# The roots of the token blocks by a power on GpSimd, and their decay matmul over split exponents

## The chip, the cores and the metric

The kernel runs on one core of a Trainium2 chip. The metric is the device time of one launch in microseconds (us). The engines are TensorE (PE, with its weight loads as PEld), VectorE (DVE), ScalarE (ACT), GpSimd (POOL) and SyncE (SP). Each follows its own program; they meet only through semaphores.

## The reference, cut to what matters

16 sequences of 256 tokens with 128 features go through four layers. Each layer's output is added to its input and normalized:

```
x = layernorm(x + mamba(x))                # state-space layer, 4 heads of 64, 128 states
x = layernorm(x + gated_expert_attention(x))   # 8 heads of 64, 8 experts, causal
x = layernorm(x + linear_attention(x))     # 16 heads of 8, rotary, gelu
x = layernorm(x + soft_experts(x))         # 64 experts x 32 slots
```

Two pieces of the state-space layer matter here. Its decay is exp of sums of dt * A over the steps between two tokens, and its output is normalized by a root, as are the layer norms:

```
dA = exp(dt * A)
h  = h * dA_t + dt_t * x_t B_t
y  = y * rsqrt(mean(y * y) + 1e-5) * norm_w
layernorm(y) = (y - mean) * rsqrt(var + eps) * w + b
```

## The kernel before, in words

`token_blocks` computes the first three layers; `soft_experts` computes the fourth. Within `token_blocks` a sequence has two chunks of 128 tokens (C = 2). The layers run as a pipeline over the sequences, one "slot" per sequence: slot t works on the state-space layer of sequence t (names with a_), on the attention of t-1 (b_), on its output turn of t-2 and on the linear attention of t-3 (c_). The slots up to 2 are written out by hand as a start, with the constants' loads and the step sizes of all sequences (`dt_steps`) between them. Then come slots 3 to 16. The order of the work on each of the five engines is written out by hand, the same in each slot (from slot 15 on pieces of the next sequence, such as its convolution, are left out, since there is none). Nothing reorders it: an instruction whose semaphores are not there holds all that is behind it on its engine.

The names that the change and the steps of the prediction touch:

- `newton` (L60) computes 1/sqrt of a 128x2 tile, on GpSimd: v = var * scale + eps (L64), an integer seed (L66), then three steps of four instructions (L80, L82, L84, L86). That is 14 instructions, each with a wait for the one before. It is called for `rms` (the state-space norm, from `ssq`), `ln` (twice a slot: ln1 and ln2), `lnB`, `lnC`, `lnD`, six times a slot.
- The decay: `a_all` holds the step exponents (-dt*A) of all sequences. `a_am` on GpSimd (L2208) spreads one chunk's four columns to a masked 128x512 tile `am` in the arena, one affine_select for each chunk. `a_seg` on TensorE (L529) multiplies it with the lower triangle `low_s` in f32, a single 128x512 matmul per chunk, which gives the sums of the exponents; the trace shows it as two records. ScalarE then takes the exponential (L1226).
- `b_vg` on GpSimd (L2225) multiplies the values of the attention by their gates, two passes of 128x512 (`vals`).
- `a_mx` (L2218), `a_xb` (L2235), `c_km` (L2248, L2250) and `c_turn` (L2242) are GpSimd's other work in a slot.
- On VectorE: the convolution taps (L1581, six pairs a slot), the rotary products `c_qr` (L1771, L1776: its output `qr` goes to the transposes L785 on TensorE), the gated output `mo` (L1741), `kv` (L1781, needed by TensorE's L799), the residual `ra` (L1644, which reads the `rms` root), `na` (L389) and `x` (L1664), which read the ln roots.
- `arena` is one SBUF tile in which the a_ work has its areas.

Of the kernel before, what the change touches and what calls it, by code (L numbers as in the profile page):

```python
# [15 lines left out]
P = 128  # L16
# [43 lines left out]
def newton(pool, wait_apart, done, k, source, var, scale, eps, v, y, t, fused=False):  # L60


    wait_apart(pool, source)
    pool.tensor_scalar(v[:], var, scale, eps, ALU.mult, ALU.add).then_inc(done, 1)  # L64
    wait_apart(pool, (done, k + 1))
    pool.tensor_scalar(y[:].bitcast(I32), v[:].bitcast(I32), -0.5, RSQRT_SEED,  # L66
                       ALU.mult, ALU.add).then_inc(done, 1)
    if fused:
        for s in range(RSQRT_STEPS):
            wait(pool, done, k + 2 + 3 * s)  # L70
            pool.scalar_tensor_tensor(t[:], y[:], -0.5, y[:], ALU.mult, ALU.mult).then_inc(done, 1)
            wait(pool, done, k + 3 + 3 * s)
            pool.tensor_tensor(t[:], t[:], v[:], ALU.mult).then_inc(done, 1)
            wait(pool, done, k + 4 + 3 * s)
            pool.scalar_tensor_tensor(y[:], t[:], 1.5, y[:], ALU.add, ALU.mult
                                      ).then_inc(done, 1 if s < RSQRT_STEPS - 1 else 1 + RSQRT_STEPS)
        return
    for s in range(RSQRT_STEPS):
        wait(pool, done, k + 2 + 4 * s)
        pool.tensor_tensor(t[:], y[:], y[:], ALU.mult).then_inc(done, 1)  # L80
        wait(pool, done, k + 3 + 4 * s)
        pool.tensor_tensor(t[:], t[:], v[:], ALU.mult).then_inc(done, 1)  # L82
        wait_apart(pool, (done, k + 4 + 4 * s))
        pool.tensor_scalar(t[:], t[:], -0.5, 1.5, ALU.mult, ALU.add).then_inc(done, 1)  # L84
        wait(pool, done, k + 5 + 4 * s)
        pool.tensor_tensor(y[:], y[:], t[:], ALU.mult).then_inc(done, 1)  # L86


def build(nc, x, xT, in_wT, conv_w, conv_b, dt_bias, A_log, Dh, norm_w, out_wT, ln_w, ln_b,
          w_q, w_k, w_gate, v_exp, o_exp, WqkvT, bq, bk, bv, gamma, beta, phi, W, b_exp,  # L90
          ident, causal, neg_blocks, strict_low, upper, head_of, rot, cosT, sinT, w8,
          out):
    x3_dram = nc.dram_tensor("x3_tok", (NB * L, D), F32, kind="Internal").ap()
    x3T_dram = nc.dram_tensor("x3_T", (D, NB * L), F32, kind="Internal").ap()
    ctx = ExitStack()
# [14 lines left out]
def token_blocks(nc, kept, x, xT, in_wT, conv_w, conv_b, dt_bias, A_log, Dh, norm_w, out_wT, ln_w, ln_b,  # L110
# [3 lines left out]

    HELD = NB - 3

    AREAS = dict(cin=(NCH, L + TAPS - 1), cacc=(NCH, L), xbc=(NCH, L), am=(C, NH, P), lx=(C, NH, P), mx=(C, NH, P),
                 xd=(C, NH, HD), xD=(C, NH, HD), tz=(C, DI), sz=(C, DI), ya=(C, DI), yg=(C, DI), yT=(2, L),
                 xt_in=(2, L), x_in=(2, C, D))
    arena = kept.enter_context(nc.sbuf_tensor("arena", [P, sum(math.prod(shape) for shape in AREAS.values())], F32))  # L120
    area, at = {}, 0
    for name, shape in AREAS.items():
# [13 lines left out]
    with ExitStack() as ctx:  # L136
        def sb(name, shape, dt=F32):
            return ctx.enter_context(nc.sbuf_tensor(name, [P] + shape, dt))
# [2 lines left out]
            return kept.enter_context(nc.semaphore(name))  # L141


        id_f = sb("id_f", [P])
        id_b = sb("id_b", [P], BF16)
        fill = sb("fill", [L], BF16)
        id_r = sb("id_r", [P], F32R)
        causal_s = sb("causal_s", [P])
        negb_f = sb("negb_f", [3, P])
        negb = sb("negb", [3, P], BF16)  # L150
        low_s = sb("low_s", [P])
        upp_s = sb("upp_s", [P])
        hof = sb("hof", [P])
        hof_n = sb("hof_n", [P])
# [3 lines left out]
        sin_s = sb("sin_s", [L])  # L158
        w8_s = sb("w8_s", [NE])
        in_w = sb("in_w", [2 * DI + 2 * D + NH])  # L160
        out_w0 = sb("out_w0", [2, D])
        out_w = sb("out_w", [2, D])
        cw0 = sb("cw0", [NCH, TAPS])
        cb0 = sb("cb0", [NCH])
# [31 lines left out]
        bet = sb("bet", [D])  # L196


        sv = sb("sv", [TT, NH])
        sa = sb("sa", [TT, NH])  # L200
        su = sb("su", [TT, NH])
        sd = sb("sd", [TT, NH])
        s2 = sb("s2", [TT, NH])
        sp = sb("sp", [TT, NH])
        ea = sb("ea", [NH])
        dt_all = sb("dt_all", [TT, NH])
        a_all = sb("a_all", [TT, NH])


        xt_in = area["xt_in"]  # L210
# [4 lines left out]
        xd = area["xd"]  # L215
        xD = area["xD"]
        btok = sb("btok", [P])
        gm = sb("gm", [C, P])
        am = area["am"]
        lx = area["lx"]  # L220
        mx = area["mx"]
        ep = sb("ep", [NH])
# [7 lines left out]
        sq = sb("sq", [DI])  # L230
        ssq = sb("ssq", [C])
        yT = area["yT"]
        ra = sb("ra", [C, D])
        na = sb("na", [C, D])
        xb = sb("xb", [C, D])
        x1 = sb("x1", [C, D])
# [17 lines left out]
        rg = sb("rg", [C, HB])  # L254
        rgS = sb("rgS", [C, 2, DH])
        rgb = sb("rgb", [C, P])
        oT = sb("oT", [2, C, HP, P])

        mo = ve_f[:, 0:MO * HP * P].rearrange("p (s a n) -> p s a n", s=MO, a=HP)
        oa = sb("oa", [L])  # L260
# [91 lines left out]
        CONV_PREP = 4  # L352
        PREP = CONV_PREP + 10
        DT_PARTS = [slice(0, C), slice(C, TT)]
        DT_OPS = LOG1P_TERMS + 10
        DT_TILES = [range(C), range(C, C + 8), range(C + 8, C + 16), range(C + 16, C + 23), range(C + 23, TT)]
        VE_PARTS = 4

# [20 lines left out]

        def rsqrt(pool, n, b, scale, eps, source, per, fused=False):  # L380
            _, _, v, y, t = nbuf[n]
            newton(pool, wait_both, norms[n]["rstd"], RSQRT_OPS * b, (source, per * b + per), var_of(n), scale, eps,
                   v, y, t, fused)

        def scale_rows(dve, n, src, dst, b):

# [85 lines left out]
        def _(pe):  # L472
# [43 lines left out]
            def a_seg(b, c):  # L516

                if c == 0:
                    if b == 1:
                        pe.wait_ge(q["a_r"], C * b)  # L520
                    if b not in (1, 2):
                        pe.wait_ge(q["a_sz"], b + 1)
                    if b > 1:
                        pe.wait_ge(q["a_x1h"], b)
                        pe.wait_ge(q["a_x1l"], b)
                else:
                    pe.wait_ge(q["a_lx"], C * b + 1)
                pe.wait_ge(q["a_am"], C * b + c + 1)
                pe.matmul(ps_a[:, :], low_s[:], am[:, c, :, :].rearrange("p h t -> p (h t)"),  # L529
                          start=True, stop=True, skip_group_check=True).then_inc(q["a_seg_ps"], 1)  # L530

            def a_xt(b):
                pe.wait_ge(q["a_xbc"], b + 1)
# [458 lines left out]
            a_z(0, 0)  # L992
            a_xbc(1, 1, 0, 0)
            pe.wait_ge(ready, READY)
            a_seg(0, 0)
            dt_rows(1)
            a_seg(0, 1)
# [192 lines left out]
        def _(act):  # L1190
# [50 lines left out]
            def a_sq(b):  # L1241

                act.wait_ge(q["a_yg"], b + 1)
                for c in range(C):
                    if c == 1:
                        act.wait_ge(q["a_sq"], C * b + 1)
                    nc.scalar.activation(sq[:], yg[:, c, :], ACT.Square, scale=0.5, accum_out=ssq[:, c:c + 1]
                                         ).then_inc(q["a_sq"], 1)

            def a_yt(b):  # L1250
# [104 lines left out]
            def dt_exps(n):  # L1355
                act.wait_ge(dts, DT_OPS * n + 2)
                nc.scalar.activation(su[:, DT_PARTS[n], :], sa[:, DT_PARTS[n], :], ACT.Exp, scale=-1.0
                                     ).then_inc(dt_exp, 1)

            def slot(r, u, a, b, o, c, more):  # L1360
                t = 2 * r + u
                if a:
# [204 lines left out]
        def _(dve):  # L1567
# [303 lines left out]

            def dt_steps(n):
                rows = DT_PARTS[n]
                dve.wait_ge(dt_exp, n + 2)
                V.tensor_scalar(sd[:, rows, :], su[:, rows, :], 2.0, None, ALU.add).then_inc(dts, 1)
                dve.wait_ge(dts, DT_OPS * n + 3)
                V.reciprocal(sd[:, rows, :], sd[:, rows, :]).then_inc(dts, 1)
# [7 lines left out]
                for k in range(LOG1P_TERMS - 1, 0, -1):  # L1885
# [12 lines left out]
                V.scalar_tensor_tensor(a_all[:, rows, :], dt_all[:, rows, :], -1.0,  # L1898
                                       ea[:].unsqueeze(1).to_broadcast([P, rows.stop - rows.start, NH]), ALU.mult, ALU.mult
                                       ).then_inc(dts, 1)  # L1900
                dve.wait_ge(dts, DT_OPS * n + DT_OPS)

            def slot(r, u, a, b, o, c, more):
                t = 2 * r + u
# [122 lines left out]
            dt_steps(0)  # L2027
            a_conv(0, 0, (2,))
            a_sz(0)
            a_conv(0, 0, (3,))  # L2030
            a_conv(0, 1, (1,))
            a_conv(0, 1, (2,))
# [165 lines left out]
        @block.gpsimd  # L2198
        def _(pool):
            G = nc.gpsimd  # L2200

            def a_am(b):

                if b < 2:
                    pool.wait_ge(dts, DT_OPS * (b + 1))
                for c in range(C):
                    wait(pool, q["a_seg_ps"], C * b)
                    G.affine_select(out=am[:, c, :, :], in_=a_all[:, b * C + c, :].unsqueeze(2).to_broadcast([P, NH, P]),  # L2208
                                    compare_op=ALU.is_ge, fill=0.0, base=0, pattern=[[0, NH], [1, P]],
                                    channel_multiplier=-1).then_inc(q["a_am"], 1)  # L2210

            def a_mx(b):

# [844 lines left out]
```

## Time and profile before

| | before |
|---|---|
| times of three runs | 1496.85, 1499.70, 1500.32 us |
| median | 1499.7 us |
| span of the profiled execution | 1497.5 us |
| PE busy | 1440.1 us (96%) |
| DVE busy | 1218.1 us (81%) |
| ACT busy | 821.0 us (55%) |
| POOL busy | 751.1 us (50%) |
| `token_blocks` / `soft_experts` | up to about 1004 us / the rest |

For the profiled execution only its span is given; no time of its own stands beside it. The span runs from the first to the last instruction. "Busy" counts the time in which an engine computes. PEclk is the TensorE clock that was granted as a share of full speed. A row "idle before <-ENGINE name" says how long an engine sat and what let it go on. In the three runs the time varies by 3.5 us.

### The profile page before, as it was taken

The page shows a single profiled execution, that of the slowest core. Times are in us where ns is not written, and L with a number is a line of the kernel's source. Part 1 is how long each engine was busy: PE and PEld are TensorE (multiplying, and loading weights), DVE is VectorE, ACT ScalarE, POOL GpSimd, SP SyncE. Part 2 cuts the span into 40 slices and gives each one's busy share as a digit, 9 for nine tenths or more (in the row PEclk, how much of TensorE's full clock was granted, in tenths as well). Part 3 has the DMA queues.
Part 4 walks back from the last instruction along what each step waited for, and adds up shares of the span by engine and source line. Part 5 has one row for each costly group of instructions (what it writes and reads, how often), then busy time and mean ns, then how long its engine had stood idle before and what let it go on. Part 6 is the DMA issues. An engine that isn't in the chain of part 4 may idle for free. (4 is left out here: it accounts for less than half of the span.)

```text
span 1497.5 us, 32591 instructions
## 1 busy us (share of the span) xinstructions
PE 1440.1 (96%) x10940; PEld 1269.0 (85%) x10940; DVE 1218.1 (81%) x2359; ACT 821.0 (55%) x1850; POOL 751.1 (50%) x1833
## 2 busy tenths in 40 slices
PE   8889999999999999999999999987999999998998
PEld 6658888888888888888888887867999999998997
DVE  5778889889898898898898887768888888857664
ACT  4354454555454455455554544315777767677775
POOL 1433346355354454453463452226777777457772
PEclk8789999999999999999999999998999999999999
DMA  5100000000000000000000003006777777887872
GB/s 193 60 8 8 1 15 2 15 16 1 15 5 12 15 5 12 15 1 15 16 1 15 9 1 127 1 1 166 188 187 192 196 192 192 263 335 296 310 304 75
DMA packets 135426, 130.43 MB, mean 87 GB/s; under 512 B 7232, under 2 KB 125248, under 8 KB 128768
## 3 DMA queue, kind: packets, MB, share of 16 engines
q1 hardware_dynamic: 135296, 128.79, 27.8%
q8 instruction: 70, 1.15, 0.3%
q14 instruction: 60, 0.49, 0.1%
HBM read 72.93 MB, written 55.84 MB: 86 GB/s over the span
## 5 line engine op out<-in xcount | busy, mean ns | idle before, releaser
L737 PE MATMUL ps_l<-ve_f,oe 128*128 128x128 f32 x2048 | 275.7, 279 | 0.8 <-DVE ve_f L1741 0.8
L737 PEld LDWEIGHTS ps_l<-ve_f,oe 128*128 128x128 f32 x2048 | 248.8, 192 | 23.1 <-issue 20.5
L1741 DVE SCALAR_TENSOR_TENSOR ve_f<-ps_s,oT 128x512 f32<-128x512 f32 x248 | 166.4, 679 | 4.1 <-PE ps_l L737 2.3
L2935 POOL TENSOR_TENSOR d_s<-d_ex 128x1024 f32<-128x1024 f32 x31 | 125.3, 4041 | 83.2 <-ACT d_ex L2685 83.2
L1702 DVE COPY_PREDICATED vals<-oh,ps_l 128x1024 f32<-128x1024 int32 x112 | 146.8, 1311 | 17.2 <-PE ps_l L477 15.1
L2560 PE MATMUL ps_s<-d_ex,arena 128*128 128x128 f32 x1024 | 121.5, 278 | 7.0 <-DVE d_ex L2828 7.0
L2560 PEld LDWEIGHTS ps_s<-d_ex,arena 128*128 128x128 f32 x1024 | 118.7, 194 | 7.4 <-DVE d_ex L2828 7.4
L475 PE MATMUL ps_l<-veH,x1H 128*128 128x512 f32 x256 | 115.4, 451 | 0.8 <-DVE vals L1702 0.7
L1293 ACT ACTIVATE ve_f<-ps_l,r 128x128 f32<-128x128 f32 x128 | 47.3, 369 | 125.7 <-DVE r L1714 125.4
L2548 PE MATMUL ps_l<-arena 128*128 (+1 forms) x960 | 112.2, 275 | 2.3 <-ACT d_raw L2680 2.3
L2548 PEld LDWEIGHTS ps_l<-arena 128*128 128x128 f32 x960 | 109.6, 192 | 2.5 <-ACT d_raw L2680 2.5
L64 POOL TENSOR_SCALAR lnB_v<-lnB_mv 128x2 f32<-128x2 f32 x15 | 2.9, 193 | 213.5 <-DVE lnB_mv L378 213.5
L477 PE MATMUL ps_l<-veH,x1L 128*128 128x512 f32 x256 | 101.0, 395 | 0.0
L476 PE MATMUL ps_l<-veL,x1H 128*128 128x512 f32 x256 | 100.5, 393 | 0.0
L2810 DVE TENSOR_REDUCE d_nm<-ps_l 128x128 f32<-128x2048 f32 x31 | 71.0, 2291 | 32.7 <-PE ps_l L2548 28.5
L1192 ACT ACTIVATE pt<-ps_l 128x384 f32<-128x384 f32 x128 | 62.7, 494 | 62.4 <-PE ps_l L675 61.1
L2737 ACT ACTIVATE e_prT<-ps_l 128x512 f32<-128x512 f32 x128 | 72.5, 595 | 38.8 <-PE ps_l L2603 38.8
L2856 DVE TENSOR_REDUCE e_nmx<-e_lt 128x1 f32<-128x2048 f32 x32 | 73.0, 2282 | 19.1 <-DMA e_lt<-logits 18.1
L1581 DVE SCALAR_TENSOR_TENSOR arena<-arena,cw 128x256 f32<-128x256 f32 x192 | 85.7, 489 | 1.2 <-ACT arena L1192 1.1
L2603 PE MATMUL ps_l<-d_id,e_lt 128*128 128x128 f32 x512 | 77.9, 276 | 6.4 <-ACT e_lt L2729 6.4
L2676 ACT ACTIVATE d_raw<-ps_l 128x512 f32<-128x512 f32 x120 | 67.1, 603 | 20.9 <-DVE d_nm L2810 9.3
L2828 DVE TENSOR_TENSOR d_ex<-d_ex,d_sr 128x2048 f32<-128x2048 f32 x32 | 74.7, 2335 | 1.1
(332 smaller groups left out, 3865.8 us busy)
## 6 DMA issues: line engine op xcount, KB each, us to landing
logits<-d_raw SPq DMA_DIRECT2D x128, 256.0 KB, 3.5
e_lt<-logits SPq DMA_DIRECT2D x32, 1024.0 KB, 5.2
y_slots<-d_ys SPq DMA_DIRECT2D x64, 256.0 KB, 4.6
d_ex<-y_slots SPq DMA_DIRECT2D x8, 1024.0 KB, 6.9
e_y<-y_slots SPq DMA_DIRECT2D x6, 1024.0 KB, 6.8
d_w<-W SPq DMA_DIRECT2D x16, 256.0 KB, 3.4
arena<-xT SPq DMA_DIRECT2D x16, 128.0 KB, 2.4
arena<-x SPq DMA_DIRECT2D x16, 128.0 KB, 2.5
```

The lines of the kernel that those rows point to most:

```text
L475: pe.matmul(ps, lh, rh, start=first, stop=False, skip_group_check=True)
L476: pe.matmul(ps, lh, rl, start=False, stop=False, skip_group_check=True)
L477: return pe.matmul(ps, ll, rh, start=False, stop=last, skip_group_check=True)
L737: last = pe.matmul(ps_u[:, cols], oe[:, hp, e, :], mo[:, n % MO, hp, :], start=False, stop=(e == NE - 1 and hp == HP - 1), skip_group_chec ...
L1581: V.scalar_tensor_tensor(cacc[:, ch, :], cin[:, ch, tap:tap + L], cw[:, ch, tap:tap + 1], cacc[:, ch, :], ALU.mult, ALU.add).then_inc(q["a ...
L1702: V.copy_predicated(vals[:], oh[:, :, :, e:e + 1].bitcast(I32).to_broadcast([P, C, HB, DH]), ps_v[e % 2][:].rearrange("p c (h k) -> p c h ...
L1741: V.scalar_tensor_tensor(mo[:, n % MO, :, :].rearrange("p a n -> p (a n)"), chosen_of(b, c), float(NE - e), oT[:, u, c, :, :].rearrange("p ...
L2548: last = pe.matmul(home_of(g)[:, k, i, :], xtf[:, b, c, :], phf[:, cols], start=(i == 0), stop=(i == BB - 1), skip_group_check=True)
L2560: last = pe.matmul(sl[:, k, i, :], xs[:, (BK * i + k) * C + c, :], ex[:, u, c, k, i, :], start=(c == 0 and i == 0), stop=(c == C - 1), ski ...
L2603: last = pe.transpose(tp[:, k, j * P:(j + 1) * P], lt[:, u, c, 4 * k + j, :], id_f[:])
L2828: V.tensor_tensor(part, part, sr[:].unsqueeze(1).to_broadcast([P, NB, P]), ALU.mult).then_inc(q["mult"], 1)
L2935: G.tensor_tensor(s8[:], part[:, 0:8, :], part[:, 8:16, :], ALU.add).then_inc(n, 1)
```

## The change

It does three things. First, the unfused roots (`rms`, `ln` twice, `lnB`, `lnC`, `lnD`) are computed by two GpSimd instructions, v = var + eps and y = v ** half, where `half` is a tile of -0.5. The mean in `rms` moves into the scale of the square on ScalarE. The fused roots on VectorE and those of `soft_experts` stay. Second, each f32 matmul of `a_seg` becomes two f32r matmuls that accumulate: over `a_high`, the exponents rounded to f32r (ScalarE), and over `a_rest`, what the rounding left (VectorE). So GpSimd spreads four tiles a slot in place of two, and `am` gets a place of its own. `a_high` and `a_rest` are computed for sequence 0 and for all the others in the start. Third, some tiles move in memory (`gm`, `ra` into the arena, the tiles of the step sizes, `negb_f` and `out_w0` into the still unused `oT`).

```
+def root(pool, wait_apart, done, k, source, var, eps, half, v, y):
+    wait_apart(pool, source)
+    pool.tensor_scalar(v[:], var, 1.0, eps, ALU.mult, ALU.add).then_inc(done, 1)
+    wait_apart(pool, (done, k + 1))
+    pool.tensor_tensor(y[:], v[:], half[:], ALU.pow).then_inc(done, RSQRT_OPS - 1)
...
+        oT = sb("oT", [2, C, HP, P])
+        half = sb("half", [C])
+        low_r = sb("low_r", [P], F32R)
+        a_high = sb("a_high", [TT, NH], F32R)
+        a_rest = sb("a_rest", [TT, NH], F32R)
+        am = sb("am", [2, C, NH, P], F32R)
...
         def rsqrt(pool, n, b, scale, eps, source, per, fused=False):
+            if fused:
+                newton(pool, wait_both, norms[n]["rstd"], RSQRT_OPS * b, (source, per * b + per), var_of(n), scale, eps,
+                       v, y, t, fused)
+            else:
+                root(pool, wait_both, norms[n]["rstd"], RSQRT_OPS * b, (source, per * b + per), var_of(n), eps,
+                     half, v, y)
...
-                pe.wait_ge(q["a_am"], C * b + c + 1)
-                pe.matmul(ps_a[:, :], low_s[:], am[:, c, :, :].rearrange("p h t -> p (h t)"),
-                          start=True, stop=True, skip_group_check=True).then_inc(q["a_seg_ps"], 1)
+                pe.wait_ge(q["a_am"], 2 * (C * b + c + 1))
+                for k in range(2):
+                    last = pe.matmul(ps_a[:, :], low_r[:], am[:, k, c, :, :].rearrange("p h t -> p (h t)"),
+                                     start=(k == 0), stop=(k == 1), skip_group_check=True)
+                last.then_inc(q["a_seg_ps"], 1)
...
+            pe.wait_ge(dt_exp, 3)
             a_seg(0, 0)
...
+            def a_rounded(n):
+                act.wait_ge(dts, DT_OPS * (n + 1) - 1)
+                copy(a_high[:, DT_PARTS[n], :], a_all[:, DT_PARTS[n], :]).then_inc(dt_exp, 1)
...
             a_tz(0)
+            act.wait_ge(ready, READY)
+            copy(low_r[:], low_s[:]).then_inc(dt_exp, 1)
+            a_rounded(0)
             a_lx(0, 0)
...
             a_tz(1)
+            a_rounded(1)
             a_cin(2, 1)
...
+            def a_left(n):
+                rows = DT_PARTS[n]
+                dve.wait_ge(dt_exp, 2 * n + 4)
+                V.tensor_tensor(a_rest[:, rows, :], a_all[:, rows, :], a_high[:, rows, :].bitcast(F32), ALU.subtract
+                                ).then_inc(dts, 1)
...
             a_sz(0)
+            a_left(0)
             a_conv(0, 0, (3,))
...
             dt_steps(1)
             a_ln1(0)
+            a_left(1)
...
                 for c in range(C):
                     wait(pool, q["a_seg_ps"], C * b)
+                    for k, part in enumerate((a_high, a_rest)):
+                        G.affine_select(out=am[:, k, c, :, :],
+                                        in_=part[:, b * C + c, :].unsqueeze(2).to_broadcast([P, NH, P]),
+                                        compare_op=ALU.is_ge, fill=0.0, base=0, pattern=[[0, NH], [1, P]],
+                                        channel_multiplier=-1).then_inc(q["a_am"], 1)
```

GpSimd's order in a slot, from the rotary product (`wq_f` is its tile) over the spread of the exponents and the `rms` root to `b_vg` and the ln1 root, is before:

```order
L2242 TENSOR_TENSOR wq_f<-ql,cos_s 128x512
L2208 AFFINE_SELECT arena<-a_all 128x512 x2
L64 TENSOR_SCALAR rms_v<-ssq 128x2
L66 TENSOR_SCALAR rms_y<-rms_v 128x2
L80 TENSOR_TENSOR rms_t<-rms_y 128x2
L82 TENSOR_TENSOR rms_t<-rms_t,rms_v 128x2
L84 TENSOR_SCALAR rms_t<-rms_t 128x2
L86 TENSOR_TENSOR rms_y<-rms_y,rms_t 128x2
...
L2225 TENSOR_TENSOR vals<-vals,gx 128x512 x2
L64 TENSOR_SCALAR ln_v<-ln_mv 128x2
```

and in the changed kernel, at the same place:

```order
L2277 TENSOR_TENSOR wq_f<-ql,cos_s 128x512
L2242 AFFINE_SELECT am<-a_high 128x512
L2242 AFFINE_SELECT am<-a_rest 128x512
L2242 AFFINE_SELECT am<-a_high 128x512
L2242 AFFINE_SELECT am<-a_rest 128x512
L93 TENSOR_SCALAR rms_v<-ssq 128x2
L95 TENSOR_TENSOR rms_y<-rms_v,half 128x2
L2260 TENSOR_TENSOR vals<-vals,gx 128x512 x2
L93 TENSOR_SCALAR ln_v<-ln_mv 128x2
L95 TENSOR_TENSOR ln_y<-ln_v,half 128x2
```

Between the rotary product and the `vals` pair there were two selects and 14 small instructions, and there are now four selects and two small instructions.

ScalarE's order in the start, around the first copy of `a_high` for the later sequences (`a_tz(1)`, then `a_cin(2, 1)`), is before:

```order
L1192 ACTIVATE veH<-ve_f 128x1024
L1214 ACTIVATE arena<-ps_l 128x512 [waits a_sz,a_z_ps]
L1206 ACTIVATE arena<-ps_s,cb,cw 128x256 [waits a_conv,a_xbc_ps]
L1206 ACTIVATE arena<-ps_s,cb,cw 128x256
L1192 ACTIVATE arena<-ps_s 128x2x256
```

and in the changed kernel:

```order
L1209 ACTIVATE veH<-ve_f 128x1024
L1231 ACTIVATE arena<-ps_l 128x512 [waits a_sz,a_z_ps]
L1209 ACTIVATE a_high<-a_all 128x120 [waits dt_rows]
L1223 ACTIVATE arena<-ps_s,cb,cw 128x256 [waits a_conv,a_xbc_ps]
L1223 ACTIVATE arena<-ps_s,cb,cw 128x256
L1209 ACTIVATE arena<-ps_s 128x2x256
```

The three instructions of `a_cin(2, 1)` now stand behind a copy that waits for VectorE's step sizes.

## Rows read from the trace of the kernel before

**Rows 1.** A slot's window: length, busy PE PEld DVE ACT POOL, granted clock, DMA.
```profile
506.87:564.57 57.70, 57.46 (x414) 47.84 (x413) 51.04 (x120) 29.81 (x83) 27.69 (x94) 1.00 0.04 10
```

**Rows 2.** TensorE's longest waiting line from 120 to 900 us: total, times, longest.
```profile
PE ps_s L791 <- ACT kr L1192: 2.0, 12, 0.2
```

**Rows 3.** TensorE's timeline around the two `a_seg` matmuls of a slot (start, duration).
```profile
506.87 1.13 PE L529 MATMUL ps_s<-arena,low_s 128*128 128x512 f32 x2
507.93 0.39 PE L720 MATMUL ps_s<-ohT,pick 64*128 64x128 bf16 x4
...
509.65 1.10 PE L529 MATMUL ps_s<-arena,low_s 128*128 128x512 f32 x2
510.59 0.38 PE L747 MATMUL ps_s<-id_f,oa 128*128 128x128 f32 x2
...
515.91 0.40 PE L476 MATMUL ps_l<-veL,x1H 128*128 128x512 f32 x1
516.14 0.40 PE L477 MATMUL ps_l<-veH,x1L 128*128 128x512 f32 x1
```

**Rows 4.** GpSimd's timeline in the same slot, spread, root and values.
```profile
531.54 1.22 POOL L2208 TENSOR_SCALAR_AFFINE_SELECT arena<-a_all 128x512 f32<-128x512 f32 x2
...
534.62 0.70 POOL L86 TENSOR_TENSOR rms_y<-rms_y,rms_t 128x2 f32<-128x2 f32 x1
...
538.01 2.04 POOL L2225 TENSOR_TENSOR vals<-vals,gx 128x512 f32<-128x512 f32 x2
```

**Rows 5.** VectorE's timeline beside it, from its last write of `vals`.
```profile
530.17 1.33 DVE L1702 COPY_PREDICATED vals<-oh,ps_l 128x1024 f32<-128x1024 int32 x1 [0.30 <-PE ps_l L477]
...
532.78 0.87 DVE L1581 SCALAR_TENSOR_TENSOR arena<-arena,cw 128x256 f32<-128x256 f32 x2
533.85 0.69 DVE L1771 TENSOR_TENSOR ve_f<-ps_s,sin_s 128x512 f32<-128x512 f32 x1 [0.20 <-PE ps_s L779]
534.57 0.69 DVE L1776 TENSOR_TENSOR qr<-ve_f,wq_f 128x512 f32<-128x512 f32 x1
535.18 0.87 DVE L1581 SCALAR_TENSOR_TENSOR arena<-arena,cw 128x256 f32<-128x256 f32 x2
...
537.97 0.28 DVE L1781 TENSOR_TENSOR kv<-ps_s,hof_n 128x128 f32<-128x128 f32 x1
```

**Rows 6.** Two operations of VectorE beside GpSimd's selects and values, and one alone.
```profile
13.91 1.72 DVE L1581 SCALAR_TENSOR_TENSOR arena<-arena,cw 128x256 f32<-128x256 f32 x2
13.95 1.41 POOL L2208 TENSOR_SCALAR_AFFINE_SELECT arena<-a_all 128x512 f32<-128x512 f32 x2 [13.43 <-DVE a_all L1898]
93.06 2.04 DVE L389 TENSOR_SCALAR na<-ra,ln_mv,ln_y 128x128 f32<-128x128 f32 x2 [0.44 <-POOL ln_y L86]
92.98 2.05 POOL L2225 TENSOR_TENSOR vals<-vals,gx 128x512 f32<-128x512 f32 x2
544.82 0.61 DVE L389 TENSOR_SCALAR na<-ra,ln_mv,ln_y 128x128 f32<-128x128 f32 x2
```

**Rows 7.** TensorE's timeline where it takes `qr` and `kv`, and the wait of its loads.
```profile
535.32 0.20 PEld L785 LDWEIGHTS ps_s<-id_f,qr 128*128 128x128 f32 x2 [0.31 <-DVE qr L1776]
...
538.63 0.39 PE L799 MATMUL ps_s<-kv,qr 128*128 128x128 f32 x2
```

**Rows 8.** GpSimd's groups from 120 to 900 us: busy, mean ns.
```profile
L82 POOL TENSOR_TENSOR ln_t<-ln_t,ln_v 128x2 f32<-128x2 f32 x84 | 21.5, 256 | 6.6
...
L2208 POOL TENSOR_SCALAR_AFFINE_SELECT arena<-a_all 128x512 f32<-128x512 f32 x26 | 15.9, 636 | 0.0
```

**Rows 9.** The start: TensorE, ScalarE and VectorE from 49 us.
```profile
49.22 1.13 PE L512 MATMUL ps_s<-in_w,arena 128*128 128x256 f32 x4 [0.61 <-ACT arena L1192]
59.22 0.69 PE L598 MATMUL ps_s<-id_f,x 128*128 128x128 f32 x2 [3.26 <-DVE x L1664]
48.54 0.63 ACT L1192 ACTIVATE arena<-ps_s 128x512 f32<-128x512 f32 x1
49.19 0.28 DVE L1898 SCALAR_TENSOR_TENSOR a_all<-dt_all,ea 128x120 f32<-128x120 f32 x1
```

More of the change, by code:

```diff
@@ L115, in token_blocks @@
     HELD = NB - 3
-    AREAS = dict(cin=(NCH, L + TAPS - 1), cacc=(NCH, L), xbc=(NCH, L), am=(C, NH, P), lx=(C, NH, P), mx=(C, NH, P),
+    AREAS = dict(cin=(NCH, L + TAPS - 1), cacc=(NCH, L), xbc=(NCH, L), lx=(C, NH, P), mx=(C, NH, P),
                  xd=(C, NH, HD), xD=(C, NH, HD), tz=(C, DI), sz=(C, DI), ya=(C, DI), yg=(C, DI), yT=(2, L),
-                 xt_in=(2, L), x_in=(2, C, D))
+                 xt_in=(2, L), x_in=(2, C, D), gm=(C, P), ra=(C, D))
     arena = kept.enter_context(nc.sbuf_tensor("arena", [P, sum(math.prod(shape) for shape in AREAS.values())], F32))
@@ L141, in sem @@
             return kept.enter_context(nc.semaphore(name))
+        oT = sb("oT", [2, C, HP, P])
+        early = oT[:, :, :, :].rearrange("p u c a n -> p (u c a n)")
+        steps = early[:, 0:6 * TT * NH].rearrange("p (k n h) -> p k n h", k=6, n=TT)
+        sv, sa, su, sd, s2, sp = (steps[:, k, :, :] for k in range(6))
+        negb_f = early[:, 768:768 + 3 * P].rearrange("p (k n) -> p k n", k=3)
+        out_w0 = early[:, 1280:1280 + 2 * D].rearrange("p (j d) -> p j d", j=2)
         id_f = sb("id_f", [P])
         id_b = sb("id_b", [P], BF16)
+        half = sb("half", [C])
         fill = sb("fill", [L], BF16)
@@ L148, in token_blocks @@
         causal_s = sb("causal_s", [P])
-        negb_f = sb("negb_f", [3, P])
         negb = sb("negb", [3, P], BF16)
         low_s = sb("low_s", [P])
+        low_r = sb("low_r", [P], F32R)
         upp_s = sb("upp_s", [P])
@@ L160, in token_blocks @@
         in_w = sb("in_w", [2 * DI + 2 * D + NH])
-        out_w0 = sb("out_w0", [2, D])
         out_w = sb("out_w", [2, D])
@@ L196, in token_blocks @@
         bet = sb("bet", [D])
[L199 to L204, printed above, removed]
         ea = sb("ea", [NH])
@@ L217, in token_blocks @@
         btok = sb("btok", [P])
-        gm = sb("gm", [C, P])
-        am = area["am"]
+        gm = area["gm"]
         lx = area["lx"]
@@ L232, in token_blocks @@
         yT = area["yT"]
-        ra = sb("ra", [C, D])
+        ra = area["ra"]
         na = sb("na", [C, D])
@@ L256, in token_blocks @@
         rgb = sb("rgb", [C, P])
-        oT = sb("oT", [2, C, HP, P])
         mo = ve_f[:, 0:MO * HP * P].rearrange("p (s a n) -> p s a n", s=MO, a=HP)
@@ L354, in token_blocks @@
         DT_PARTS = [slice(0, C), slice(C, TT)]
-        DT_OPS = LOG1P_TERMS + 10
+        DT_OPS = LOG1P_TERMS + 11
         DT_TILES = [range(C), range(C, C + 8), range(C + 8, C + 16), range(C + 16, C + 23), range(C + 23, TT)]
@@ L381, in rsqrt @@
             _, _, v, y, t = nbuf[n]
-            newton(pool, wait_both, norms[n]["rstd"], RSQRT_OPS * b, (source, per * b + per), var_of(n), scale, eps,
-                   v, y, t, fused)
+            if fused:
[4 more added lines that the diff above has]
+                     half, v, y)
         def scale_rows(dve, n, src, dst, b):
@@ L1246, in a_sq @@
                         act.wait_ge(q["a_sq"], C * b + 1)
-                    nc.scalar.activation(sq[:], yg[:, c, :], ACT.Square, scale=0.5, accum_out=ssq[:, c:c + 1]
+                    nc.scalar.activation(sq[:], yg[:, c, :], ACT.Square, scale=0.5 / math.sqrt(DI), accum_out=ssq[:, c:c + 1]
                                          ).then_inc(q["a_sq"], 1)
@@ L1873, in dt_steps @@
                 rows = DT_PARTS[n]
-                dve.wait_ge(dt_exp, n + 2)
+                dve.wait_ge(dt_exp, 3 * n + 2)
                 V.tensor_scalar(sd[:, rows, :], su[:, rows, :], 2.0, None, ALU.add).then_inc(dts, 1)
@@ L1900, in dt_steps @@
                                        ).then_inc(dts, 1)
-                dve.wait_ge(dts, DT_OPS * n + DT_OPS)
+            def a_left(n):
[3 more added lines that the diff above has]
+                                ).then_inc(dts, 1)
             def slot(r, u, a, b, o, c, more):
@@ L2200, in _ @@
             G = nc.gpsimd
+            G.memset(half[:], -0.5)
             def a_am(b):
@@ L2207, in a_am @@
                     wait(pool, q["a_seg_ps"], C * b)
-                    G.affine_select(out=am[:, c, :, :], in_=a_all[:, b * C + c, :].unsqueeze(2).to_broadcast([P, NH, P]),
-                                    compare_op=ALU.is_ge, fill=0.0, base=0, pattern=[[0, NH], [1, P]],
-                                    channel_multiplier=-1).then_inc(q["a_am"], 1)
+                    for k, part in enumerate((a_high, a_rest)):
[3 more added lines that the diff above has]
+                                        channel_multiplier=-1).then_inc(q["a_am"], 1)
             def a_mx(b):
```

## The prediction, made before the result

> **What bounds the kernel now.** I read the page's busy times first (they are in the table above), then the window of one slot, then TensorE's waits, then the timelines of GpSimd, VectorE and TensorE side by side. TensorE computes in 96% of the span. In a slot it is busy for 57.46 of 57.70 us at full clock, and VectorE for 51.04 [rows 1]. Its worst waiting line has 2.0 us in 780 us [rows 2]. So TensorE sets the slot's length, and two things count: what TensorE itself has less to do, and whether what it reads comes later. VectorE has only 6.66 us to spare per slot (57.70 - 51.04), and they lie in a few places. GpSimd has 30 us to spare. Its work costs nothing by its length, only by what it does to VectorE beside it.
>
> **The decay matmul.** The first `a_seg` of a slot takes from 506.87 to the next start at 507.93, 1.06 us; the second takes 509.65 to 510.59, 0.94 [rows 3]. A 128x512 matmul of the rounded kind takes 0.23 from start to start (515.91 to 516.14). Two for each chunk are 0.46, and an f32 matmul ahead may add some 0.05. The saving is 2.00 less about 1.05, **0.95 us per slot**. VectorE must follow, out of its 6.66 us of idle time a slot; where it can't, a part is lost. All times below are in the old slot's clock, after this shift. That bears on slots 2 to 15, 14 in all: 14 x 0.95 = 13.3 us, if nothing comes late.
>
> **The four selects and the roots on GpSimd.** A select takes 0.64 [rows 8], so two more take 1.2 per slot. A root loses 12 small instructions of about 0.2 us. That chain ran from the selects' end near 532.8 to the `vals` pair at 538.01 [rows 4], 5.2 us. The power on 128x2 is nowhere in this trace. It can't well be shorter than the product of the same size, 0.2 to 0.26 [rows 8]. Above, I bound it by the chain it replaces, 5 us. I take 0.3, near the product of the same shape, and keep both ends. None of the six roots makes anyone wait before (TensorE's waits name none), so their shortening gives nothing by itself. What it does is to move what is queued behind them on GpSimd. The `vals` pair has its input at 530.17 + 1.33 = 531.5 [rows 5], and only GpSimd's order holds it. It will start at 532.7 + 1.2 + 0.5 for the two instructions of the root, plus waits: about 534.9 in place of 538.01.
>
> **What lies there on VectorE.** Two engines that both read tiles in SBUF stand in each other's way here. A pair of convolution taps takes 0.87 alone [rows 5] and 1.72 beside two selects [rows 6], +0.85. A pair of `na` takes 0.61 alone and 2.04 beside the `vals` pair, +1.43 [rows 6]. Beside it GpSimd's pair took 2.05 against 2.04 [rows 4], so VectorE pays all of it. At 538.01 the `vals` pair lay beside `kv` and `ra`, which read PSUM, and cost nothing. The Trainium skill, in "Trainium Architecture — The Big Picture", section "What this means for kernel authors", calls the port pair that VectorE shares with GpSimd an exclusive lock and no split of bandwidth. Rows 6 agree; by that rule without a number each of VectorE's operations could wait for a whole pass, which would give more than the sum here.
>
> In the new slot the third and fourth select (532.7 to 533.9) lie on the pair of taps at 532.78. It ends 0.85 later, at 534.5. Of that 0.20 go into VectorE's old wait ahead of L1771 [rows 5], so it is 0.65 late. Then the `vals` pair (534.9 to 537) lies on `qr`, which before began at 534.57 and now near 535.2, and on the pair of taps behind it. I put that at the +1.43 of `na`. So `kv`, before done at 537.97 + 0.28 = 538.25, ends 0.65 + 1.43 = 2.08 later. TensorE took it at 538.63, a slack of 0.38 [rows 7]. TensorE stands **1.7 us** there. It stands earlier already, at the transposes of `qr`, where it had no slack at all (the load waited 0.31 for it [rows 7]); that wait is part of the same 1.7, since what follows is then late too. Between L785 and L799 nothing that TensorE has queued can be done ahead.
>
> Does later work give it back? GpSimd's later part of the slot is lighter, but no one waited for it. The selects and the convolution stand in the slots 3 to 14, 12 in all: each is -0.95 + 1.70 = **+0.75**, in sum +9.0. Slot 2 keeps its -0.9. Slot 15 has no next sequence to spread, so I count -0.6. The last slots I count at -0.2.
>
> **The start.** TensorE's first `a_seg` now waits for the copy of `low_s`, the rounding, the rest and four selects for sequence 0. I put it 0.8 us later, of which the cheaper pair gives 0.4 back before sequence 0 goes on: +0.4. Then `a_rounded(1)` on ScalarE waits for the step exponents that VectorE ends at 49.19 + 0.28 = 49.47, and `a_cin(2, 1)` behind it, which was done at 48.54 + 0.63 = 49.17, comes at about 51 [rows 9]. TensorE's L512 at 49.22 waits for it, 1.8 us. But TensorE then waits 3.26 us for `x` at 59.22 anyway [rows 9], and the root ahead of `x` is shorter, so this is hidden. If this cover is gone, it costs those 1.8. On VectorE `a_left` is a product-sized instruction (0.28 as L1898) in a stretch with idle time. Start in all: +0.5, between -3 (the shorter roots at 59 us let `x` come before) and +3. The moves in memory change no order and I price them at nothing.
>
> **Sum.** +9.0 - 0.9 - 0.6 - 0.2 + 0.5 = +7.8. The profiled execution's span is 1497.5; it becomes 1505.3. The median of the runs is 2.2 above that span, so the forecast is 1499.7 + 7.8 = **1507.5 us**. Its own range: the delay per slot may be 1.2 to 2.4 in place of 1.7, so the slot is worth +0.25 to +1.45, in sum (12 of them, with -1.2 for the rest) +1.8 to +16.2, 1501.5 to 1516.
>
> **Rivals.**
>
> *A, faster.* VectorE holds its place against GpSimd. For it: while `qr` ran, a small GpSimd instruction beside it took 0.70 in place of some 0.2 [rows 4, 5, 8], so there it was GpSimd that stood. Then the `vals` pair fits into the gaps of L1771 and `mo`, which read PSUM, and `kv` is late by the selects alone or not at all. It decides at a delay of `kv` under 0.38 + 0.95 = 1.33. With no delay at TensorE: 14 x -0.95 = -13.3, **1486.4**. Against: rows 6, where GpSimd's long passes won twice.
>
> *B, heavier.* Each of VectorE's operations waits for a full pass. `qr` begins near 535.2 beside a pass that ends at 536 and ends at 536.5, 1.25 late; the taps meet the second pass and lose 1.0 more. 0.65 + 1.25 + 1.0 - 0.38 = 2.5, so +1.55 a slot, x12 = 18.6, less 1.2: +17.4, **1517**. The power may take part in it, if it holds the port too.
>
> *C, even.* Only one pass of the `vals` pair meets an operation that it hinders, the other falls beside L1771 or `mo`. This fits a power of 0.8 to 1.5 us as well. 0.65 + 0.72 - 0.38 = 1.0: the gain and the loss cancel, and -1.2 is left: **1498.5**. If the power is over 3 us, the pair stays near 538, only the selects cost (0.65 - 0.38 = 0.27), and the slot gains 0.68: 1490. That is the far end of the power's range.
>
> That the change doesn't do what it says I don't count: the order shows the two instructions in place of 14 at each root.
>
> **Chances.** Forecast 0.43, A 0.22, C 0.20, B 0.15. A measurement of this kernel tells 0.3% from no change, 4.5 us, so "same" is 1495.2 to 1504.2. From the forecast I put 0.05 there and 0.01 below, from C 0.15 there, 0.03 faster and 0.02 slower. Slower: 0.37 + 0.15 + 0.02 = 0.54. Same: 0.20. Faster: 0.22 + 0.03 + 0.01 = 0.26. The range reaches from A to B's upper side, 1485 to 1519.
>
> **What would show it.** Two `a_seg` records of one chunk from start to start 0.46 to 0.55 (the gain). The `vals` pair 3 us earlier, ahead of `kv` and no longer beside it. A pair of taps at 1.7 in place of 0.87 beside the third and fourth select, and `qr` or the taps behind it longer by 1.4 in sum. TensorE waiting in every slot at L785 and L799's successors for `qr` and `kv`, about 1.7 us. Slots of 58.45 us against 57.70. If the slot measures 56.75, A holds; if `vals` still lies beside `kv`, the power is long. Wrong altogether would be a GpSimd that becomes late itself, with TensorE waiting for `am`, or a clock under full in the slots.

## The result, and the profile after

The changed kernel takes 1521.53 us (median of 4, 1517.9 to 1524.54) against 1498.73 before: ratio 1.0151, interval 1.013 to 1.0172. It is slower, as forecast, but by 22.8 us where 7.8 were forecast, and it lies above the range.

The page's busy times of the changed kernel, the order of columns as in the table of before:

```profile
span 1522.7 us, 31606 instructions
...
PE 1439.7 (95%) x10940; PEld 1278.1 (84%) x10940; DVE 1246.3 (82%) x2361; ACT 821.0 (54%) x1853; POOL 569.3 (37%) x750
```

GpSimd has 182 us less to do (751.1 before), VectorE is busy 28 us longer with two instructions more. TensorE is busy as long as before, though its decay matmuls are cheaper: some of its work ran at a lower clock.

TensorE's waits from 120 to 900 us (total, times, longest), where before the worst line had 2.0 us [rows 2]:

```profile
PE ps_s L815 <- DVE kv L1806: 18.7, 12, 1.6
PE ps_s L801 <- DVE qr L1801: 6.7, 12, 0.6
PE ps_s L560 <- DVE arena L1627: 3.3, 13, 0.3
```

Each slot now has three waits. (L560 takes the `xd` products of VectorE, `a_xd` in the code, the convolved input times the step sizes and times `d_h`.) Two slots that follow each other, from `kv` to `kv` (length, busy PE PEld DVE ACT POOL, granted clock), beside the 57.70 of [rows 1]:

```profile
550.31:611.07 60.76, 58.39 (x412) 49.24 (x412) 53.13 (x120) 29.86 (x83) 15.72 (x24) 0.97 0.03 10
611.07:670.18 59.11, 56.74 (x412) 47.66 (x412) 53.03 (x120) 29.79 (x83) 15.71 (x24) 1.00 0.03 10
```

There are two kinds of slot. A slot at full clock is 59.11 long, 1.41 more than before. The other is 60.76 long, 1.65 more again, and TensorE is busy for just those 1.65 us more. Where the time lies is seen in one window of 3.2 us in such a slot, and in a window of 4.0 us of the other slot, near the same place:

```profile
552.20:555.40 3.20, 3.20 (x17) 3.13 (x17) 2.84 (x10) 0.80 (x2) 1.58 (x3) 0.50 0.00 0
...
612.20:616.20 4.00, 4.00 (x37) 3.42 (x36) 3.83 (x16) 0.80 (x2) 1.81 (x4) 1.00 0.00 0
```

The granted clock is 0.50 there, the lower of its two levels (1.2 GHz), right behind TensorE's longest wait of the slot. It happens in 7 slots (behind the `kv` at 249.8, 369.7, 430.5, 550.3, 670.2, 731.0 and 850.8). Before, the clock was full from 103 to 997 us.

GpSimd's timeline at the place of [rows 4]:

```profile
543.02 0.64 POOL L2242 TENSOR_SCALAR_AFFINE_SELECT am<-a_high 128x512 fp32r<-128x512 f32 x1
543.61 0.82 POOL L2242 TENSOR_SCALAR_AFFINE_SELECT am<-a_rest 128x512 fp32r<-128x512 f32 x1
544.52 0.24 POOL L93 TENSOR_SCALAR rms_v<-ssq 128x2 f32<-128x2 f32 x1
544.91 0.72 POOL L95 TENSOR_TENSOR rms_y<-rms_v,half 128x2 f32<-128x2 f32 x1
545.59 2.53 POOL L2260 TENSOR_TENSOR vals<-vals,gx 128x512 f32<-128x512 f32 x2
```

The power takes 0.69 to 0.72. The `vals` pair takes 2.53 where it took 2.04 [rows 4]. VectorE's timeline beside it, which answers to [rows 5] (532.78 there is 543.05 here, 10.27 later):

```profile
543.05 1.65 DVE L1606 SCALAR_TENSOR_TENSOR arena<-arena,cw 128x256 f32<-128x256 f32 x2
544.63 0.68 DVE L1796 TENSOR_TENSOR ve_f<-ps_s,sin_s 128x512 f32<-128x512 f32 x1
545.34 0.69 DVE L1801 TENSOR_TENSOR qr<-ve_f,wq_f 128x512 f32<-128x512 f32 x1
545.95 2.45 DVE L1606 SCALAR_TENSOR_TENSOR arena<-arena,cw 128x256 f32<-128x256 f32 x2
...
550.31 0.27 DVE L1806 TENSOR_TENSOR kv<-ps_s,hof_n 128x128 f32<-128x128 f32 x1
```

The first pair of taps, beside the third and fourth select, takes 1.65 in place of 0.87. The second pair, beside the `vals` pair, takes 2.45 in place of 0.87, while `qr` itself is not stretched: it began 0.25 ahead of the pair. `kv` ends 2.06 later against the taps' start than before. TensorE's rows, for [rows 7]:

```profile
546.09 0.44 PE L801 MATMUL ps_s<-id_f,qr 128*128 128x128 f32 x2 [0.56 <-DVE qr L1801]
...
550.64 0.49 PE L815 MATMUL ps_s<-kv,qr 128*128 128x128 f32 x2 [1.56 <-DVE kv L1806]
```

And the decay pairs of a slot at full clock, for [rows 3]:

```profile
637.45 0.74 PE L544 MATMUL ps_s<-am,low_r 128*128 128x512 f32 x2
638.12 0.39 PE L736 MATMUL ps_s<-ohT,pick 64*128 64x128 bf16 x4
...
639.83 0.71 PE L544 MATMUL ps_s<-am,low_r 128*128 128x512 f32 x2
640.46 0.41 PE L763 MATMUL ps_s<-id_f,oa 128*128 128x128 f32 x2
...
645.02 0.33 PE L560 MATMUL ps_s<-id_f,arena 128*128 128x128 f32 x1 [0.25 <-DVE arena L1627]
```

A pair takes 0.67 and 0.63 to the next start, where 1.06 and 0.94 stood. It saves 0.70 a slot. The second chunk's part of that, 0.31, is lost 5 us later in the wait at L560; hold_am and hold_am_xd below test this.

**The bill of the profiled executions** (1522.7 - 1497.5 = 25.2). From `kv` to `kv` the first 11 slots take 25.2 us more (from 190.72 to 850.78, against 191.65 to 826.55): 11 x 1.41 = 15.5 and 6 falls of the clock of 1.65 = 9.9. The next slot is 1.2 longer with one more fall in it (57.07 against 55.86), the one after it 1.1 shorter. The start is 0.9 shorter (190.72 against 191.65). `soft_experts` and the end make 0.8 more.

### The profile page after: what moved, and what is told of

It is laid out like the page before. It is cut to its first block and busy times, and to the rows that moved or that the text cites. A ratio compares the mean times of both kernels' runs of the same rounds, so it can differ in the third digit from the quotient of the medians.

```text
span 1522.7 us, 31606 instructions
## 1 busy us (share of the span) xinstructions
PE 1439.7 (95%) x10940; PEld 1278.1 (84%) x10940; DVE 1246.3 (82%) x2361; ACT 821.0 (54%) x1853; POOL 569.3 (37%) x750
## 5 line engine op out<-in xcount | busy, mean ns | idle before, releaser
L753 PE MATMUL ps_l<-ve_f,oe 128*128 128x128 f32 x2048 | 284.6, 284 | 0.8 <-DVE ve_f L1766 0.8
L753 PEld LDWEIGHTS ps_l<-ve_f,oe 128*128 128x128 f32 x2048 | 257.3, 197 | 23.1 <-issue 14.4
L1606 DVE SCALAR_TENSOR_TENSOR arena<-arena,cw 128x256 f32<-128x256 f32 x192 | 114.1, 636 | 1.1 <-ACT arena L1209 1.0
```

The lines of the kernel that those rows point to most:

```text
L753: last = pe.matmul(ps_u[:, cols], oe[:, hp, e, :], mo[:, n % MO, hp, :], start=False, stop=(e == NE - 1 and hp == HP - 1), skip_group_chec ...
L1606: V.scalar_tensor_tensor(cacc[:, ch, :], cin[:, ch, tap:tap + L], cw[:, ch, tap:tap + 1], cacc[:, ch, :], ALU.mult, ALU.add).then_inc(q["a ...
```

## The experiments

The theory: GpSimd's `vals` pair and two more selects now lie beside operations of VectorE that read two SBUF tiles, VectorE is late at `qr` and `kv`, and TensorE, standing there, also loses its clock in some slots ("place" and "clock"). The rivals: the split decay costs it, the power costs it by its own 0.69 us, or the long slots have another cause. All times beside a run are medians; the ratio is to the kernel before on the same chip. The moves in memory, the third part of the change, weren't tried alone. They are in split_newton and in hold_am_xd too, whose slots are 58.0 and 56.9 long, so they don't make the slots of 59 to 61.

**roots_only.** The kernel before with `root` in place of the unfused `newton`, nothing else:

```
-            newton(pool, wait_both, norms[n]["rstd"], RSQRT_OPS * b, (source, per * b + per), var_of(n), scale, eps,
-                   v, y, t, fused)
...
+                root(pool, wait_both, norms[n]["rstd"], RSQRT_OPS * b, (source, per * b + per), var_of(n), scale, eps,
+                     half, v, y)
```

> The kernel before with the power roots alone; the decay matmul stays one f32 matmul over two selects a chunk pair. Theory (place): the vals pair of GpSimd moves up from beside kv to beside qr and the convolution taps, VectorE is late at qr and kv, TensorE waits some 1.3 to 1.8 us a slot there, and where it stood long its clock falls for a while (1.65 us more in such a slot). Slot 59.0 to 60.8 us against 57.7; total 1513 to 1527. Rival (the split is to blame: two more selects and two matmuls): 1497 to 1500, slots 57.7.

1506.93, ratio 1.0057 (1.0039 to 1.0075). All slots are 58.75, +1.05, no fall of the clock. TensorE's waits:

```profile
PE ps_s L813 <- DVE kv L1795: 9.2, 12, 0.8
PE ps_s L799 <- DVE qr L1790: 7.4, 13, 0.6
```

The roots alone make the slots longer, by the two waits foreseen, 1.4 us a slot in all. (Of the 1.4 a part was there before: the wait of 0.17 a slot at L791 [rows 2] is gone.) The slot and the total are under what was expected: the clock held, and the start was 4.4 us shorter (first `kv` at 187.26).

**split_newton.** The changed kernel with the old roots:

```
-                root(pool, wait_both, norms[n]["rstd"], RSQRT_OPS * b, (source, per * b + per), var_of(n), eps,
-                     half, v, y)
...
+            newton(pool, wait_both, norms[n]["rstd"], RSQRT_OPS * b, (source, per * b + per), var_of(n), scale, eps,
+                   v, y, t, fused)
```

> The changed kernel with the old 14-instruction roots; the decay matmul stays split over four selects. Theory (place): the vals pair starts near its old place beside kv and costs nothing; the decay pair saves 0.4 us a slot, the selects make qr some 0.5 late, of which TensorE has about 0.4 back before kv. Slot 57.3 to 57.7, no fall of the clock; total 1493 to 1500. Rival (the split is to blame): slots of 59 us and more, 1515 or more.

1502.99, ratio 1.0036 (1.0018 to 1.0053). Slots of 57.7 to 58.2, most 58.0, no fall of the clock. A little over what I expected. The split alone is not the cause of slots of 59 and more, but it is no gain either: TensorE waits 7.1 us in 12 slots for `qr`, 0.59 each. The roots alone add 1.05 a slot and the split alone 0.3, together near the 1.41 of the changed kernel at full clock.

**fill_before_kv.** The changed kernel, and TensorE multiplies zeros where it would stand. The fills write into the other half of the PSUM bank in which the attention's output is summed, and they change that output:

```
                 if c:
+                    if more:
+                        awake(bank[1][:, 1, :], 12)
                     c_out(t - 3)
```

> The changed kernel with 12 bf16 matmuls of 128x256 by a zero tile on TensorE ahead of its wait for kv, in a half bank of PSUM that nobody reads: TensorE computes while it would stand. Theory (clock): no fall of the clock in the slots, all slots 59.1 to 59.3, total 1510 to 1514. Rival (the long slots come from something else than TensorE's standing still): still six slots near 60.8, total 1521 or more.

1512.84, ratio 1.0101 (1.0084 to 1.0117). No slot of 60.8 is left: they are 59.1 to 59.4, at clock 1.00 from 120 to 900 us. The wait for `kv` became the fill; the other stayed:

```profile
543.02 1.47 PE L498 MATMUL ps_l<-fill 128*128 128x256 bf16 x12
544.74 0.49 PE L815 MATMUL ps_s<-kv,qr 128*128 128x128 f32 x2 [0.25 <-DVE kv L1808]
```

Work that does nothing made no slot longer than 59.4, and 8.7 us of the total went. So without TensorE's standing at `kv` the clock doesn't fall. That a wait of this length isn't enough by itself is seen below.

**hold_vals.** The changed kernel, and the `vals` pair waits for `kv`:

```
                 if b:
+                    if c:
+                        pool.wait_ge(q["c_kv"], t - 2)
                     b_vg(t - 1)
```

> The changed kernel with one wait more: GpSimd starts the vals pair only when VectorE has done kv, from slot 3 on; the four selects stay where they are. Theory (place): the pair lies beside kv and ra again, no cost; slots 57.3 to 57.7, no fall of the clock, total 1493 to 1500. Rival (the power itself or the selects cost it): 1510 or more.

1495.36, ratio 0.9985 (0.9969 to 1.0001), which can't be told from the kernel before. All slots are 57.8, just over the 57.7 that I expected at most, no fall of the clock. A wait added to an engine took 26 us off the changed kernel's 1521.53. The slot is 1.35 shorter than its full-clock slot. What it has over the 57.30 of hold_am below is the selects' part, the wait at `qr`:

```profile
PE ps_s L801 <- DVE qr L1801: 6.7, 12, 0.6
PE ps_s L560 <- DVE arena L1627: 2.9, 13, 0.2
PE ps_l L691 <- ACT ve_f L1312: 2.3, 14, 0.2
```

**vals_first.** The kernel before, with no power and no split, and only GpSimd's order changed:

```
+                if b:
+                    b_vg(t - 1)
                 if a:
                     rsqrt(pool, "rms", t, 1.0 / DI, EPS, q["a_sq"], C)
-                if b:
-                    b_vg(t - 1)
```

> The kernel before with one exchange on GpSimd in every slot: the vals pair ahead of the rms root, all roots by the old 14 instructions, decay unsplit. Theory (place): the pair starts near 532.8 in the old slot and lies on the first pair of taps; qr and kv come late; slot 58.3 to 59.0, total 1506 to 1515. Rival (the power takes part in the loss, place alone doesn't do it): slots 57.7, total 1497 to 1500.

1515.41, ratio 1.0108 (1.0089 to 1.0127), slots of 58.8 to 59.1, both just over what I expected. The price of the place, without the change:

```profile
537.26 2.22 POOL L2225 TENSOR_TENSOR vals<-vals,gx 128x512 f32<-128x512 f32 x2
...
537.29 2.48 DVE L1581 SCALAR_TENSOR_TENSOR arena<-arena,cw 128x256 f32<-128x256 f32 x2
```

A pair of taps that takes 0.87 alone takes 2.48 beside the `vals` pair (+1.61, and +1.58 in the changed kernel).

**mult_for_power.** The changed kernel with a product for the power, which leaves the root out of what is computed:

```
-    pool.tensor_tensor(y[:], v[:], half[:], ALU.pow).then_inc(done, RSQRT_OPS - 1)
+    pool.tensor_tensor(y[:], v[:], half[:], ALU.mult).then_inc(done, RSQRT_OPS - 1)
```

> The changed kernel with a product in place of the power in each root (0.2 us in place of 0.69), which leaves the root out of what is computed. Theory (place): the vals pair starts some 0.5 earlier and still lies on qr and the taps: slots 58.7 to 59.2, and 60.8 where the clock falls, total 1508 to 1522. Rival (the 0.69 us of the power makes the loss): slots 57.3 to 57.8, total under 1500.

1510.21, ratio 1.0079 (1.0064 to 1.0094), slots of 58.95. The product takes 0.20 where the power took 0.72, and the slot is 0.16 shorter than 59.11: the power's length is not the cause. This time `qr` was hit first:

```profile
538.56 2.49 POOL L2260 TENSOR_TENSOR vals<-vals,gx 128x512 f32<-128x512 f32 x2
...
538.84 1.30 DVE L1801 TENSOR_TENSOR qr<-ve_f,wq_f 128x512 f32<-128x512 f32 x1
...
540.07 1.66 DVE L1606 SCALAR_TENSOR_TENSOR arena<-arena,cw 128x256 f32<-128x256 f32 x2
```

The `vals` pair began 0.28 ahead of `qr` here, and 0.25 behind it in the changed kernel. So in these two traces the one that began first kept its length. Here 0.61 fall on `qr` and 0.79 on the taps, 1.40 in all, near the 1.58. TensorE stands as long as in the changed kernel (14.2 us for `qr`, 10.0 for `kv`, together 24.2 against 25.4), in most slots in two more even parts. Its clock doesn't fall.

**hold_am.** The kernel hold_vals, and the four selects moved:

```
                     a_xb(t, u)
+                if more:
+                    a_am(t + 1)
                 if c:
                     c_km(t - 3)
                     c_turn(t - 3)
-                if more:
-                    a_am(t + 1)
```

> The kernel hold_vals (vals pair after kv) with the four selects issued ahead of the mean of k, some 12 us earlier in the slot, beside VectorE's copies out of PSUM. Theory (place): qr isn't late any more; the gain of the decay pair comes through but for what TensorE waits at the xd product: slot 57.3, total 1488 to 1492. Rival (the gain is bounded elsewhere): 57.7, total 1494 to 1497.

1489.41, ratio 0.9935 (0.9914 to 0.9956), all slots 57.30. The wait at `qr` is gone, as expected. The slot is 0.40 shorter than before the change.

**hold_am_xd.** The kernel hold_am, and on VectorE:

```
+                if a:
+                    a_xd(t)
                 if c:
                     b_res(t - 3)
-                if a:
-                    a_xd(t)
```

> The kernel hold_am with VectorE's two xd products ahead of its statistics of lnB, 0.8 us earlier. Theory: TensorE's wait of 0.25 a slot for them (L560) goes, the whole 0.70 of the decay pair counts: slot 57.0, total 1485 to 1489. Rival: what comes 0.8 later behind them (lnB, the first vals copies) is waited for instead: slot 57.3 or more.

1483.08, ratio 0.9895 (0.9881 to 0.991), slots of 56.81 to 56.94, a little under what I expected. The wait at L560 is gone. It was 0.25 long and the slot is 0.45 shorter: TensorE is also busy 0.25 less (56.57 in a slot, against 56.82 in hold_am). So the slot is 0.85 shorter than before, 0.15 more than the decay pairs save. Why is open.

Once more beside the last two kernels:

> The kernel hold_am_xd once more, beside these: 1481 to 1485, slot 56.9. It is the mate for newton_am_xd and late_rounding on the same chip.

1481.21, ratio 0.9879 (0.9864 to 0.9894). This version beats both kernels. VectorE and GpSimd at the place of the trouble, in the first of the two runs:

```profile
523.66 0.69 DVE L1801 TENSOR_TENSOR qr<-ve_f,wq_f 128x512 f32<-128x512 f32 x1
524.27 0.87 DVE L1606 SCALAR_TENSOR_TENSOR arena<-arena,cw 128x256 f32<-128x256 f32 x2
...
527.42 2.04 POOL L2260 TENSOR_TENSOR vals<-vals,gx 128x512 f32<-128x512 f32 x2 [5.45 <-DVE kv L1806]
```

GpSimd stands 5.45 us ahead of the `vals` pair, by order. Beside `kv` and `ra` the pair takes 2.04 again, and `qr` and the taps keep their 0.69 and 0.87.

**newton_am_xd.** The kernel hold_am_xd with the old roots and no added wait:

```
-                root(pool, wait_both, norms[n]["rstd"], RSQRT_OPS * b, (source, per * b + per), var_of(n), eps,
-                     half, v, y)
...
+            newton(pool, wait_both, norms[n]["rstd"], RSQRT_OPS * b, (source, per * b + per), var_of(n), scale, eps,
+                   v, y, t, fused)
...
-                    if c:
-                        pool.wait_ge(q["c_kv"], t - 2)
```

> The kernel hold_am_xd with the old 14-instruction roots (and so without the hold, which their length makes needless). Theory: in the slots the roots are hidden, slot 56.9 as with the power; only the start is some 4 to 5 us longer, as it was between split_newton (kv of slot 3 at 193.06) and hold_vals (188.09); total 1486 to 1490 against 1483 of hold_am_xd. Rival (the shorter roots give something in every slot): slots of 57.2 or more, total over 1491.

1498.28, ratio 0.9998 (0.9987 to 1.0009), against 1481.21. The theory failed and the rival held: slots of 57.4, total over 1491. The short roots give 0.55 in every slot of this order. With `xd` first, the statistics of lnB come later, and the long root behind them is no longer hidden:

```profile
521.19 0.73 DVE L401 TENSOR_SCALAR x<-ps_s,lnB_mv,lnB_y 128x128 f32<-128x128 f32 x2 [0.75 <-POOL lnB_y L86]
```

TensorE waits for it, where hold_am_xd has no such wait:

```profile
PE ps_l L487 <- DVE vals L1725: 3.6, 13, 0.3
```

Eleven times 0.55 is 6. The start is the larger part: the first `kv` of slot 3 is at 195.83 against 187.82 in hold_am_xd_again. There the clock was 0.76 of full over the first 120 us, where hold_am_xd_again had 0.83. I didn't foresee that. What lowered it wasn't tried.

**before_xd.** The kernel before with the same exchange of `a_xd` and `b_res` as in hold_am_xd.

> The kernel before with the xd products ahead of the statistics of lnB and nothing else. Theory: TensorE had no wait for them before, so nothing: slot 57.7, total 1496 to 1500. Rival (the exchange helps by itself): under 57.4, under 1495.

1501.03, ratio 1.0011 (1.0002 to 1.002), slots of 57.83. It gains nothing, by itself it costs 0.1 a slot. It pays in hold_am, where TensorE waits at L560, and not here, where it doesn't.

**late_rounding.** The kernel hold_am_xd, and in the start:

```
-            a_rounded(1)
             a_cin(2, 1)
+            a_rounded(1)
```

> The kernel hold_am_xd with the rounding of the later sequences' exponents on ScalarE behind a_cin(2, 1) in place of ahead of it. Theory: TensorE's wait of 2.6 us for that convolution input in the start goes; the selects of sequence 1 come no earlier, so part of it is waited for there: 0 to 3 us less than hold_am_xd, 1480 to 1483. Rival: the rounding comes later and x of sequence 0 with it: no difference or slower.

1485.29, ratio 0.9903 (0.9888 to 0.9918), against 1481.21 beside it: 4 slower, a miss; the rival held. The slots are the same 56.85. The first `kv` is at 192.92 against 187.82. TensorE's waits for the convolution input fell from 3.0 to 0.9 us, but those for `am` rose from 4.6 to 7.0, and the clock was 0.79 of full in the first 120 us, against 0.83. What each of the two costs isn't separated.

## Why the prediction was wrong, by its steps

**The place on VectorE: right.** I had the selects at +0.85 on the first pair of taps and the `vals` pair at +1.43 on what comes behind. Measured: +0.78 and +1.58. `kv` was to end 2.08 later and ended 2.06 later. TensorE took it 1.73 later, where I wrote 1.7 (550.64 against 538.63 + 10.28 = 548.91; by 10.28 its rotary product ahead, L779 and L795, is later). That the sum is hit so closely is luck in part: 0.65 was to come from the selects, and `qr` was 0.50 late; 1.43 was to come from the pair, and it was 1.58. GpSimd paid too, 2.53 for the pair where I had VectorE pay all of it. vals_first shows the price without the change, hold_vals takes it away.

**The decay pair, 0.95 saved per slot: the mis-sized term.** I had it at 0.95; it saves 0.70, since a pair takes 0.65 and not 0.5. I took the start-to-start time inside a run of rounded matmuls and added 0.05 for the neighbours, which no row showed. And I said that VectorE must follow. It doesn't in the stretch from the gates (`eg`, which come when TensorE's gate matmuls are done) to the `xd` products: the second `a_seg` stands behind the gate matmuls, so its 0.31 go into the wait at L560, 0.25 here. So 0.39 counted. Without the clock a slot is +1.41; I had +0.75, and 0.56 of the difference is this step. The other 0.1 I can't place. hold_am, with the place mended and the wait at L560 left, gains 0.40 a slot, just this 0.39; hold_am_xd shows that the lost part can be had, slot 57.30 to 56.85.

**The clock: the step that is missing.** This is the step that put the time above the range. I wrote that a clock under full in the slots would make the forecast wrong, and gave it no price and no chance. Seven falls of 1.65 are 11.6 of the 25.2 us. fill_before_kv shows that they don't come where TensorE doesn't stand. Without them the time would have been some 1510, inside the range. That a wait can bring a fall was to be seen in the trace before, behind the wait of 3.26 [rows 9]; how often it would come was not:

```profile
60.00:64.00 4.00, 2.78 (x13) 2.73 (x14) 4.00 (x7) 0.67 (x3) 0.00 (x0) 0.50 0.00 2
```

**The power: 0.3 assumed, 0.69 measured, with little weight.** mult_for_power: 0.16 a slot. But by those 0.4 the `vals` pair began behind `qr` and not ahead of it, as I had it. The order that I described is the one of mult_for_power.

**The start, +0.5: wrong sign.** It is 0.9 shorter at the first `kv`. The wait for `x` of 3.26 us, under which I hid the delay of the convolution input, is gone. In roots_only it is gone by the short roots; in split_newton it is gone too, with the old roots behind new waits. Two new ones came, for the convolution input (2.6 where I had 1.8) and for `am` (2.3 of it at sequence 1, which I hadn't counted):

```profile
PE ps_s L544 <- POOL am L2242: 4.7, 2, 2.4
PE ps_s L526 <- ACT arena L1209: 2.9, 2, 2.6
```

**The rivals.** A (VectorE holds its place) is refuted by the pair of taps at 2.45. C was half right in its picture: the first pass of the `vals` pair did lie beside `qr` without stretching it, but the pair's price fell on the taps in full. B gave 1517 for heavier contention. Its +1.55 a slot is near the measured 1.41 by luck: it has TensorE stand 2.5 for 1.73, and saves 0.95 for 0.39. It has no clock in it either.

## What to carry to other kernels

Making an idle engine faster moves what is queued behind it. Ask what that will lie beside, and if the old place was free, hold it there with a wait. Where TensorE is the bound, a wait of 1 to 2 us put into every slot may cost its length twice, because the clock can fall behind it, as it did here in 7 slots of 12. A saving on the bounding engine counts only up to the next place where it waits for a chain that began before the saving.

## What I had not expected of the hardware

- GpSimd's power on 128x2 takes 0.69 us against 0.20 for the product of the same shape (0.72 and 0.20 in the `rms` root).
- The clock's fall doesn't follow from the length of the waits alone. TensorE stands 0.56 and 1.56 us within 5 us in every slot of the changed kernel, and it falls in 7 of 12. In mult_for_power it stands nearly as long in all (24.2 us against 25.4), mostly in two more even waits, and it falls in none. Once, ahead of 838.89, it stands 0.56 and 1.56 there too, and the clock stays full. In vals_first it stands up to 1.6 at one place, and it falls in none. What picks the slot stays open.
- The first 120 us react to every edit by their clock (0.76 to 0.89 of full), and the first `kv` lies anywhere from 185.95 to 195.83. Two profiles of one kernel, hold_am_xd, have it at 185.95 and 187.82, so 2 us of such a difference may be chance.
